# A bias folded into a matmul, and a new order of the work, in a four-layer AdaLN/FFN kernel on one Trainium2 core

## The reference, cut to what matters

```python
# layer 0: rotate/shift each image (bilinear gather), then a ternary-weight FFN 256 -> 1024 -> 256
# layer 1: attention pooling under a mask, then 4 dense experts, two of which are combined per token
# layer 2: language adapter, layer norm, then a 256x256 frequency-domain matrix
w1, w2 = W1[language_ids], W2[language_ids]             # (128, 256, 64), (128, 64, 256)
h = relu(einsum('bsh,bha->bsa', x, w1) + b1[language_ids][:, None, :])
x2 = x + einsum('bsa,bah->bsh', h, w2) + b2[language_ids][:, None, :]
# layer 3: per-category 256x256 matrix, then a gated ternary FFN 256 -> 1024 -> 256
```

## Time and profile before

| | us |
|---|---|
| median of 3 runs | 3272.16 |
| lowest, highest | 3268.71, 3273.09 |
| the profiled execution, its own time | 3272.16 |
| span of the profiled execution | 3269.9 |
| mean granted clock of TensorE | 0.891 |

### The profile page before, as it was taken

The page is one execution under the profiler, slowest core; times in us unless marked ns, Lnnn a source line. Parts: engine busy times, 40 slices in busy tenths (PEclk is TensorE's granted clock), DMA queues, the critical chain, the costliest instruction groups (busy, mean ns, idle before and its releaser), DMA issues.

```text
span 3269.9 us, 52932 instructions
## 1 busy us (share of the span) xinstructions
PE 2747.0 (84%) x14396; PEld 2197.1 (67%) x14396; DVE 1915.7 (59%) x5747; ACT 1684.6 (52%) x2882; POOL 1462.4 (45%) x1796
## 2 busy tenths in 40 slices
PE   3028988888898888889988888899888889988896
PEld 2017767777777677777767777777677777777784
DVE  5365765656566566556665666566566556665532
ACT  0025655555555555555555555565555555655442
POOL 0476554445455544444554445455544444551100
PEclk9558998989998898899989898998889899999996
DMA  4212222211222222112222211222222112221110
GB/s 189 59 38 61 53 60 56 56 43 41 57 53 55 58 56 56 38 48 52 54 60 55 56 43 41 57 53 55 57 56 56 38 47 53 55 56 43 39 36 7
DMA packets 207649, 175.21 MB, mean 54 GB/s; under 512 B 122959, under 2 KB 164692, under 8 KB 206164
## 3 DMA queue, kind: packets, MB, share of 16 engines
q1 hardware_dynamic: 172084, 119.71, 13.6%
q0 software_dynamic: 32768, 39.91, 6.7%
q10 hardware_dynamic: 2466, 11.75, 0.9%
HBM read 152.85 MB, written 9.99 MB: 50 GB/s over the span
## 4 chain that ended last, share of the span: by engine, by line
PE 73%; SPq 10%; DVE 5%; issue 3%; POOL 3%; DMA 2%; ACT 1%; DVEq 0%; POOLq 0%; ACTq 0%
PE bank L1214 27%; PE bank L1225 24%; SPq L528 9%; PE bank L1117 5%; PE bank L1123 3%; PE bank L1105 2%; PE bank L1277 2%; PE bank L1111 2%; POOL w_win L888 2%; PE bank L1253 2%; PE bank L1264 2%; DMA c<-w_out 2%; DVE front_stats L686 1%; PE bank L1166 1%; PE bank L1181 1%
## 5 line engine op out<-in xcount | busy, mean ns | idle before, releaser
L888 POOL DMA_INDIRECT w_win<-in_windows,w_idx x1024 | 1072.3, 1047 | 412.1 <-issue 295.5
L1214 PE MATMUL bank<-c_T,moe_w 128*128 128x256 f32 x4096 | 1044.7, 401 | 0.0
L1225 PE MATMUL bank<-moe_w,moe_hidden_T 128*128 128x256 f32 x4096 | 976.5, 381 | 0.3 <-ACT moe_hidden_T L1042 0.3
L1214 PEld LDWEIGHTS bank<-c_T,moe_w 128*128 128x128 f32 x4096 | 808.7, 202 | 136.1 <-issue 23.7
L1225 PEld LDWEIGHTS bank<-moe_w,moe_hidden_T 128*128 128x128 f32 x4096 | 759.2, 190 | 126.6 <-issue 21.9
L1042 ACT ACTIVATE moe_hidden_T<-bank,moe_b 128x256 f32<-128x256 f32 x1024 | 428.4, 470 | 404.3 <-PE bank L1214 402.2
L640 DVE TENSOR_TENSOR w_prod<-w_win,w_hat 128x72 f32<-128x72 f32 x2048 | 326.6, 229 | 131.2 <-issue 130.9
L895 POOL TENSOR_SCALAR front_stats<-front_stats 128x2 f32<-128x2 f32 x32 | 6.1, 192 | 853.0 <-ACT q_front L980 852.9
L790 DVE SCALAR_TENSOR_TENSOR x_back<-bank,gates,x_back 128x256 f32<-128x256 f32 x256 | 112.0, 479 | 273.0 <-PE bank L1225 272.8
L1246 PE MATMUL bank<-xT_back,adapters 128*64 128x64 f32 x512 | 60.2, 308 | 188.6 <-ACT xT_back L1048 188.6
L1042 ACT ACT_TABLE_LOAD x126 | 161.7, 1283 | 74.0 <-PE bank L1214 72.6
(11 more groups left out here) (220 smaller groups left out, 4156.4 us busy)
## 6 DMA issues: line engine op xcount, KB each, us to landing
L_cond_W<-in_L_cond_W SPq DMA_DIRECT2D x128, 256.0 KB
adapters<-in_adapter SPq DMA_DIRECT2D x128, 192.5 KB
w_win<-in_windows,w_idx POOLq DMA_INDIRECT x1024
gamma_beta<-in_gamma_beta SPq DMA_DIRECT2D x128, 128.0 KB
moe_w<-in_moe_w ACTq DMA_DIRECT2D x2, 4096.0 KB
x_front<-in_x SPq DMA_DIRECT2D x32, 256.0 KB
c<-w_out SPq DMA_DIRECT2D x512, 16.0 KB
L_cond_b<-in_L_cond_b SPq DMA_DIRECT2D x128, 64.0 KB
```

The lines of the kernel that those rows point to most:

```text
L888: gp.indirect_dma_start(out=V[par][:, g_ * WLEN:(g_ + 1) * WLEN], out_offset=None, in_=t["windows"], in_offset=bass.IndirectOffsetOnAxis(a ...
L1214: last = te.matmul((H0, H1)[j % 2][:, (i % 2) * QT:(i % 2 + 1) * QT], moe1[:, (e * NDB + d) * F + f * P:(e * NDB + d) * F + (f + 1) * P], ...
L1225: last = te.matmul(Y[:, u * D:(u + 1) * D], hT[:, (i % 4) * QT + u * P:(i % 4) * QT + (u + 1) * P], moe2[:, i * D:(i + 1) * D], start=(f = ...
```

## The change

The hidden layer of the adapter gets its bias on PE: b1 is stored as a row of 64 columns in partition 0 of the adapter block (which grows from 385 to 448 columns), and a matmul with one row of contraction (64 columns of b1 against 64 ones) closes each image's accumulation. The four ACT activations with a bias column become one over the whole quad. Beside this all four tables of `SLOT` are new. The order of the steps on PE becomes, with the steps of front and back marked F and B:

```diff
--- before.py
+++ after.py
@@ -50,7 +50,7 @@
 C_ID, C_MASK, C_E4, C_LOW, C_HALF = 0, P, 4 * P, 4 * P + 4, 4 * P + 20
 CCONST = 4 * P + 21
 NFB, NDB = F // P, D // P
-L2W = NDB * ADIM + D + 1
+L2W = NDB * ADIM + D + ADIM


 def ap(t, off, dims, parts=None, p0=0):
@@ -86,32 +86,33 @@

 SLOT = {
...
     "tensor": {
-        "back": (0, 2, 4, 11, 13, 15, 17, 22, 24, 28, 35, 36, 42, 43, 54, 59),
-        "experts": (1, 5, 6, 8, 9, 12, 14, 16, 19, 20, 23, 25, 26, 29, 31, 32, 33, 38, 39, 40, 41, 45, 46, 47, 48, 50,
-                    52, 55, 56, 57, 58, 60, 61, 63),
-        "front": (3, 7, 10, 18, 21, 27, 30, 34, 37, 44, 49, 51, 53, 62, 64),
+        "back": (0, 2, 5, 16, 18, 21, 25, 29, 31, 35, 39, 46, 47, 52, 58, 63),
+        "experts": (1, 3, 4, 7, 9, 10, 11, 13, 14, 15, 17, 20, 23, 24, 26, 27, 28, 33, 37, 38, 41, 42, 43, 44, 45, 51,
+                    53, 54, 55, 56, 57, 59, 60, 61),
+        "front": (6, 8, 12, 19, 22, 30, 32, 34, 36, 40, 48, 49, 50, 62, 64),
     },
 }
 DVE_STEPS, POOL_STEPS, ACT_STEPS = 120, 18, 4
@@ -1053,10 +1054,7 @@
                 back_T(q, 0, XTB)
                 yield next(at)
                 act.wait_ge(E["b_ah"], q + 1)
-                for a in range(QI):
-                    ins = s.activation(A2h[0:ADIM, a * S:(a + 1) * S], B0[0:ADIM, a * S:(a + 1) * S], ACT.Relu,
-                                       bias=A2[0:ADIM, (a + 1) * L2W - 1:(a + 1) * L2W])
-                ins.then_inc(E["b_relu"], 1)
+                s.activation(A2h[0:ADIM, :], B0[0:ADIM, 0:QT], ACT.Relu).then_inc(E["b_relu"], 1)
                 yield next(at)
                 back_T(q, 1, XTB)
                 yield next(at)
@@ -1243,8 +1241,9 @@
                     o = B0[0:ADIM, a * S:(a + 1) * S]
                     w = a * L2W
                     for d in range(NDB):
-                        last = te.matmul(o, A2[:, w + d * ADIM:w + (d + 1) * ADIM],
-                                         XTB[:, d * QT + a * S:d * QT + (a + 1) * S], start=(d == 0), stop=(d == NDB - 1))
+                        te.matmul(o, A2[:, w + d * ADIM:w + (d + 1) * ADIM], XTB[:, d * QT + a * S:d * QT + (a + 1) * S],
+                                  start=(d == 0), stop=False)
+                    last = te.matmul(o, A2[0:1, w + L2W - ADIM:w + L2W], ones[0:1, 0:S], start=False, stop=True)
                 last.then_inc(E["b_ah"], 1)
                 yield next(at)
                 pe.wait_ge(E["b_relu"], q + 1)
@@ -1352,7 +1351,7 @@
     adapter[:, :, 0:NDB * ADIM] = a["L2_cond_W1"].reshape(LANG, NDB, P, ADIM).transpose(0, 2, 1, 3).reshape(LANG, P, -1)
     adapter[:, 0:ADIM, NDB * ADIM:NDB * ADIM + D] = a["L2_cond_W2"]
     adapter[:, ADIM, NDB * ADIM:NDB * ADIM + D] = a["L2_cond_b2"]
-    adapter[:, 0:ADIM, L2W - 1] = a["L2_cond_b1"]
+    adapter[:, 0, L2W - ADIM:] = a["L2_cond_b1"]
     types = np.repeat(a["itok_B_0_2"].reshape(B // 2, 2).T, S, axis=0)
     att_b1 = np.zeros((P, 1), f32)
     att_b1[0:ADIM, 0] = a["L1_cond_b1"]

```

More of the change, by code:

```diff
@@ L88 @@
     "vector": {
[L89 to L94, removed]
@@ L95 @@
-        "experts": (38, 60, 85, 106),
+        "front": (0, 1, 2, 3, 4, 5, 6, 7, 11, 14, 15, 17, 18, 19, 20, 21, 24, 29, 30, 32, 33, 34, 35, 36, 46, 48, 62,
+                  63, 64, 65, 66, 71, 72, 73, 77, 78, 79, 80, 84, 92, 93, 94, 95, 96, 97, 98, 99, 107),
+        "back": (8, 9, 10, 13, 16, 22, 26, 37, 38, 39, 40, 41, 42, 47, 54, 55, 56, 57, 58, 59, 68, 82, 83, 85, 86, 87,
+                 88, 89, 106),
+        "warp": (12, 25, 27, 31, 43, 44, 45, 50, 51, 52, 53, 60, 61, 67, 69, 70, 74, 75, 76, 90, 91, 100, 101, 102, 103,
+                 104),
@@ L96 @@
+        "experts": (23, 49, 81, 105),
+        "coords": (28,),
     },
     "gpsimd": {
[L98 to L102, removed]
+        "gather": (0, 2, 3, 5, 9, 10, 11, 12, 13, 14, 15, 16, 17, 18, 19, 20, 21, 22, 23, 24, 25, 26, 27, 28, 29, 30,
+                   31, 32, 33, 34, 35, 36, 37),
@@ L103 @@
+        "front": (1, 6, 8),
+        "back": (4,),
+        "mask": (7,),
     },
     "scalar": {
[L105 to L108, removed]
+        "front": (0, 5, 6, 10, 13, 14, 18, 21, 23, 25, 30, 32, 34, 37, 43),
+        "back": (1, 2, 11, 15, 20, 22, 24, 27, 29, 33, 36, 39, 42),
@@ L109 @@
+        "experts": (3, 4, 7, 8, 9, 12, 16, 17, 19, 26, 28, 31, 35, 38, 40, 41),
+        "hats": (44, 45, 46, 47),
     },
     "tensor": {
-        "back": (0, 2, 4, 11, 13, 15, 17, 22, 24, 28, 35, 36, 42, 43, 54, 59),
-        "experts": (1, 5, 6, 8, 9, 12, 14, 16, 19, 20, 23, 25, 26, 29, 31, 32, 33, 38, 39, 40, 41, 45, 46, 47, 48, 50,
-                    52, 55, 56, 57, 58, 60, 61, 63),
-        "front": (3, 7, 10, 18, 21, 27, 30, 34, 37, 44, 49, 51, 53, 62, 64),
+        "back": (0, 2, 5, 16, 18, 21, 25, 29, 31, 35, 39, 46, 47, 52, 58, 63),
```

## The result

| | before | after |
|---|---|---|
| median, us | 3272.5 | 3432.7 |
| lowest, highest | 3268.7, 3273.1 | 3430.7, 3447.5 |
| ratio after/before, 95% interval | | 1.0502 [1.0471, 1.0532] |
| span of the profiled execution | 3269.9 | 3450.2 |

The change makes the kernel 5.0% slower. The profiled execution after is 20 us longer than the median after (3452.5 against 3432.7 us).

What follows compares the result with a forecast made beforehand. The loop down1, out1, store, 16 regroup issues, landing, sq, tc1, ah, then PE's work to the next down1 sets the turn. Terms sum to +4.0 us over 29 turns, 116, plus 6 at the start: 3394 us (3335 to 3445).

Steps and rivals of the forecast that it cites:

- The tail: End of PE's turn: work moved ahead of down1 leaves the gap before ah and is paid, +3.8 us a turn.
- q1p: Start of PE's turn: ah and H1 ahead of ad and q1p remove the wait for q1, -2.0 us a turn.
- The bias matmuls: In ah: four more float32 matmuls, eight instructions at half clock, +1.0 us a turn (0.6 to 1.0).
- The clock: PE behind the gap: full clock may return earlier, for ad; -0.4 us a turn (-1.7 to 0).
- ep, cp, lg: Middle of PE's turn: steps now directly in sequence, each behind an ACT copy, +1.1 us a turn.
- gu0: Front's q1p, q2p1, gu0, down1: steps wait for ACT copies one behind the other, +0.5 us a turn (0 to 1.0).
- Start: Turns -1 and 0: regroup waits for parts, which come later; some 3 us in each, 6 us.
- The last turns: Last three turns: the relu's wait goes and the bias comes, no difference.
- The cost of nothing: Larger adapter transfers, coords in the turn, hats in the gap and later gathers: no cost.
- A faster regroup: Rival: SP's 16 issues fall from 0.70 to 0.43 us each, 3269 us; chance 0.05.
- An unpaid gap: Rival: the cycle is bound elsewhere, say by DVE, so moving down1 is free, 3284 us; chance 0.03.
- New waits: Rival: DVE or ACT late at two or three middle steps, 1.5 to 3 us a turn, 3440 to 3480; chance 0.08.

Runs made afterwards that it cites:

- Number 3: Kernel after with only the end of the turn put back, down1 and out1 early again: 3343.3 us, ratio 1.0219.
- Number 2: Kernel after with the old bias (a column, four ACT activations, no bias matmul), new order kept: 3359.2 us, ratio 1.0262.
- Number 7: Kernel after with the bias matmul over all 128 partitions, 127 rows zero, instead of one: 3384.8 us, ratio 1.0337.
- number 8: Kernel after with other steps placed on PE to cover the copies before cp, lg and gu0: 3406.6 us, ratio 1.0400.
- number 10: Kernel after with tc1, the copy that releases ah, ahead of sq on ACT: 3342.4 us, ratio 1.0207.
- 4: Kernel after with SP issuing the 16 regroup transfers ahead of the store: 3211.1 us, ratio 0.9816.
- 9: Kernel before with regroup ahead of store and PE's turn starting ah, H1, ad, q1p, Y0,1, ffn0: 3029.6 us, ratio 0.9259.
- number 5: Kernel before, old order and old bias, with SP's regroup ahead of the store and nothing else: 3020.1 us, ratio 0.9220.

## Why the prediction was right

Forecast 3394 us (3335 to 3445), measured 3432.7. The mechanism was the forecast one; the size of one term was off by more than its bounds. In the mean of the 29 turns of the two profiled executions (starts of the steps on PE, us a turn):

| | forecast | measured |
|---|---|---|
| idle before ah, with the branch | +3.8 | +3.6 |
| wait for q1 | -2.0 | -2.1 |
| ah with its bias | +1.0 | +2.1 |
| clock: q1p, ad, H1, ffn0, Y0,1 | -0.4 | -0.8 |
| waits before cp, lg, gu0 | +1.6 | +2.0 |
| work of PE in the rest of the turn | 0 | +0.8 |
| sum | +4.0 | +5.6 |

The 29 turns hold 163 us, the start 13 and the end 5, together the 180 us between the two profiled executions. The medians are 160 us apart; only the one execution after was traced, so which rows of the table its 20 us are in is not known.

- **The tail, +3.8 a turn.** The gap grew by 3.0 us in the two turns shown (8.18 to 11.21, 6.99 to 9.95), 0.8 less than the 3.77 us of moved work, since the stretch from out1 to ah was 14.5 instead of 15.25 us (SP's 10.46 us of issue); SP was not as quick in every turn, and in the mean it grew by 3.6. Number 3 gave 3.1 a turn for putting it back. Right.
- **q1p, -2.0.** Right: q1 is ready at 1649.30 and not waited for.
- **The bias matmuls, +1.0: the step that was mis-sized.** I priced eight instructions of one row by those of 128 rows in ah, 0.123 us each; they took 0.20, and made their neighbours slower: ah grew by 2.11 us. Number 2 puts the whole at 2.5 a turn with the clock. Number 7 shows that the single row is the reason: with 128 rows the bias costs 0.9 us a turn, about what I had priced. The 1.1 to 1.5 us a turn too little, 32 to 44 us, are the main part of the 38.7 us between 3394 and 3432.7. The upper bound that I had taken, 1.0, was no bound, as no row had a matmul of one row.
- **The clock, -0.4.** About that in ad (1.50 us in this turn and 1.0 in the next, 1.9 before; 0.66 less in the mean); H1 gave some back (3.71 against 3.28; 0.22 in the mean), and q1p and ffn0, no longer right behind a wait, were quicker too.
- **ep, cp, lg, +1.1, and gu0, +0.5.** 0.46 + 0.68, to the hundredth what turn -1 showed, and 0.91. The steps beside these waits also take longer from start to start (cp 1.15 instead of 0.89 us, ep 0.38 instead of 0.22, lg and the gu steps 0.3 us more together), which is most of the 0.8 us that the table has under the rest of the turn: a bare copy costs more than its idle time. Right on PE; but removing the waits is worth 0.9 us in that kernel (number 8), as a wait for comb2 and a later clock take the rest.
- **Start, +6.** The first ah came 12.9 us later (343.97 against 331.10), the regroup of turn 0 took 28.28 us against 24.44. Right in kind, half in size. The last turns, put at no difference, are 4.6 us longer from the last ah of a full turn to the end (216.3 against 211.7): the two ah in them take 2.5 and 3.1 us, where they took 1.1 us each; the waits for relu that go there did not make up for it.
- **The cost of nothing.** The single relu costs and brings nothing in the old order that could be told apart; parts did end ahead of comb3, by 0.94 us. hats in the gap cost nothing here, and number 10 shows them in the way once the gap is used.
- **Rivals.** A faster regroup: no, 0.65 us an issue instead of 0.70, where 0.25 less was needed. An unpaid gap: refuted by numbers 3, 4 and 10. New waits: only the ones forecast.

## What to carry to other kernels

Find the loop that closes a turn across all queues, the transfer queue among them, and ask of each piece of work on which side of its gap it stands: here 3.8 us of matmuls and two lines of SP's queue decided more (+3.1 us a turn and -7.6 to -8.7 us a turn) than the operation that the change was about. An added matmul was free in a wait and dear outside it, and one of a single row among those of 128 rows was dearer than one filled up with zeros. Before a wait is removed, look at which engine is next: in numbers 8 and 9 PE then waited for DVE instead, for a part of the gain in the one and for all of it in the other. And look at the clock behind the gap, which took more of the gain in number 8 than DVE did.

## What the runs showed of the hardware

- A float32 matmul of one row by 64 columns between matmuls of 128 rows took 0.20 us an instruction at half clock; with 127 rows of zeros added it took 0.105, and the eight weight matmuls around it also ran faster (ah 2.75 us instead of 4.08, number 7).
- SP issued the same 16 transfers behind the store in 10.46 us in most turns of most kernels where the loop does not branch, but in 10.9 to 11.5 us in such turns of the loop in the kernel before, and in 10.8 to 13.2 us in the turns where the loop branches. The cause was not tried.
- PE stood 2.2 to 4.0 us at each branch of the loop, over all these kernels, with nothing to wait for in the profile; it is hidden as long as there is a gap there, and shows when the gap is gone (number 5).
